# Two transformer layers on one core: another order of the same calls on TensorE, VectorE, ScalarE and GpSimd

## The reference

```
...
        ln_out = layernorm(hidden_states, ln1_s, ln1_b)
        qkv = ln_out @ w_qkv + b_qkv
        q, k, v = jnp.split(qkv, 3, axis=-1)
        ctx = merge_heads(attention(split_heads(q), split_heads(k), split_heads(v), ltor_mask))
        attn_out = ctx @ w_ao + b_ao
        x = hidden_states + attn_out
        ln_out = layernorm(x, ln2_s, ln2_b)
        q = ln_out @ w_q + b_q
        kv = encoder_states @ w_kv + b_kv
        k, v = jnp.split(kv, 2, axis=-1)
        ctx = merge_heads(attention(split_heads(q), split_heads(k), split_heads(v), cross_mask))
        cross_out = ctx @ w_co + b_co
        x = x + cross_out
        ln_out = layernorm(x, ln3_s, ln3_b)
        mlp_out = gelu(ln_out @ w1 + b1) @ w2 + b2
        return x + mlp_out
```

## Time and profile before

| | us |
|---|---|
| median of 3 runs | 1187.67 (1187.09 to 1188.38) |
| the profiled execution, its time | 1188.55 |
| the profiled execution, its span | 1186.8 |
| PE busy | 1050.7 (89%) |
| DVE busy | 815.3 (69%) |
| ACT busy | 509.0 (43%) |
| POOL busy | 434.1 (37%) |

### The profile page before, as it was taken

One profiled execution on the slowest core, in us unless ns is written; L12 is line 12 of the kernel. 1 busy time (PEld: TensorE's weight loads), 2 busy tenths in 40 slices (PEclk: granted clock), 3 DMA queues, 4 the chain that ended last, 5 costly groups with the idle time before them and its releaser, 6 DMA issues. The chain is left out here.

```text
span 1186.8 us, 23743 instructions
## 1 busy us (share of the span) xinstructions
PE 1050.7 (89%) x9056; PEld 714.6 (60%) x9056; DVE 815.3 (69%) x1573; ACT 509.0 (43%) x954; POOL 434.1 (37%) x387
## 2 busy tenths in 40 slices
PE   7988786999999999999999999978996988888866
PEld 5876565668668668668668668656363353443524
DVE  3654776776776776776776866862448787796864
ACT  4643353464364363363373373461231434414331
POOL 2111443442442442442343343331307427264250
PEclk9988888999999999999999999989998999999988
DMA  7130100001002002102101000030000010010100
GB/s 252 62 94 23 41 1 19 24 2 38 24 2 74 23 2 82 36 2 77 55 6 33 24 18 20 9 115 18 1 27 30 1 36 21 0 38 0 36 1 18
DMA packets 38005, 41.14 MB, mean 35 GB/s; under 512 B 8640, under 2 KB 33536, under 8 KB 37648
## 3 DMA queue, kind: packets, MB, share of 16 engines
q1 hardware_dynamic: 37776, 39.54, 10.5%
q0 software_dynamic: 128, 0.10, 0.0%
HBM read 31.25 MB, written 8.39 MB: 33 GB/s over the span
## 5 line engine op out<-in xcount | busy, mean ns | idle before, releaser
L1356 DVE TENSOR_REDUCE b_neg_max<-head_area 128x16 f32<-128x1024 f32 x64 | 77.9, 1218 | 113.9 <-POOL head_area L787 113.5
L2104 POOL TENSOR_TENSOR c_rs<-c_st,head_area 128x512 f32<-128x512 f32 x64 | 88.6, 1416 | 96.8 <-DVE c_st L2583 95.9
L792 POOL TENSOR_TENSOR b_rstd<-b_var,minus_half 128x1 f32<-128x1 f32 x63 | 34.5, 548 | 241.4 <-DVE b_var L1385 241.4
L1207 ACT ACTIVATE head_area<-head_area 128x1024 f32<-128x1024 f32 x64 | 67.9, 1060 | 112.3 <-DVE head_area L1361 111.7
L1039 PE MATMUL ps<-b_hT_mlp,wl 128*128 128x512 f32 x224 | 108.3, 606 | 8.7 <-DVE b_act_g L1407 8.6
L1053 PE MATMUL ps<-w,b_act_g 128*128 128x256 f32 x448 | 104.4, 387 | 2.9 <-ACT b_act_g L1225 2.9
L787 POOL TENSOR_TENSOR head_area<-head_area,b_self_add 128x1024 f32<-128x1024 f32 x32 | 76.7, 2396 | 80.0 <-DVE head_area L1349 80.0
L787 POOL TENSOR_TENSOR head_area<-head_area 128x1024 f32<-128x1024 f32 x32 | 75.5, 2359 | 75.7 <-DVE head_area L1349 75.7
L1212 ACT ACTIVATE head_area<-ps 128x512 f32<-128x512 f32 x128 | 69.9, 598 | 72.5 <-PE ps L986 72.5
L1053 PEld LDWEIGHTS ps<-w,b_act_g 128*128 128x128 f32 x448 | 84.2, 193 | 15.6 <-ACT b_act_g L1225 3.0
L870 PE MATMUL ps<-head_area,wl 128*128 128x512 f32 x176 | 85.5, 609 | 0.0
(11 more groups left out here) (262 smaller groups left out, 2213.1 us busy)
## 6 DMA issues: line engine op xcount, KB each, us to landing
head_area<-x_mid SPq DMA_DIRECT2D x9, 512.0 KB, 3.8
wl<-in_wl SPq DMA_DIRECT2D x4, 1024.0 KB, 6.8
head_area<-in_ctxT SPq DMA_DIRECT2D x8, 512.0 KB, 3.6
x_mid<-b_x_out SPq DMA_DIRECT2D x8, 512.0 KB, 3.6
area<-in_wc SPq DMA_DIRECT2D x1, 2336.0 KB, 8.5
a_x_in<-in_x SPq DMA_DIRECT2D x16, 128.0 KB, 2.9
a_y_in<-in_ctx SPq DMA_DIRECT2D x16, 128.0 KB, 3.4
w<-in_w SPq DMA_DIRECT2D x2, 1024.0 KB, 9.4
```

What stands on the lines that cost most here:

```text
L1356: dve.tensor_reduce(neg_max[:, k % 2, :], t, AX, ALU.max, negate=True).then_inc(max_ok, 1)
L2104: pool.tensor_tensor(rs[:, i % BUFS, :], st[:, i % 3, :], rF[:, i // RS, :], ALU.mult).then_inc(rs_ok, 1)
```

## The change

The `turn` functions of PE, DVE, ACT and POOL keep the same calls with the same arguments, and every wait stays inside its call. Only the order of the calls within a turn differs. The diff, cut to its core (POOL, PE, ACT, DVE):

```
             def turn(n, prev, nxt, entry_of=None):
 
+                add_bias(prev, 6)
+
                 last_inv_std(n, 0, prev)
                 next_add_mask(n, 0, nxt)
-                add_bias(prev, 6)
...
                 next_add_mask(n, 4, nxt)
-                add_bias(n, 2)
+                next_add_mask(n, 5, nxt)
+
+                last_inv_std(n, 5, prev)
+                next_add_mask(n, 6, nxt)
+                add_bias(n, 3)
...
             def turn(n, prev, nxt):
 
+                keys_ctx(n, 0, prev)
+
                 probs_T(n, 0, nxt)
                 last_project(n, 0, prev)
-                keys_ctx(n, 0, prev)
                 times_v(n, 0)
-                next_scores(n, 0, nxt)
                 keys_ctx(n, 1, prev)
                 result_T(n, 0)
+                next_scores(n, 0, nxt)
...
                 times_v(n, 2)
                 next_scores(n, 2, nxt)
+                hidden(prev, 1, nxt)
+                norm_T_mid(n, 1)
                 hidden(prev, 2, nxt)
+                result_T(n, 2)
+                queries_mid(n, 1)
                 hidden(prev, 3, nxt)
-                result_T(n, 2)
-                norm_T_mid(n, 1)
+                last_project(n, 3, prev)
+                hidden(prev, 4, nxt)
...
                 gelu(prev, 0)
                 norm_out_mid(n, 2)
+                norm_out(0, nxt)
+                next_exps(n, 3, nxt)
                 copy_cT(n, 3)
...
-                next_maximum(n, 0, nxt)
-                next_subtract(n, 0, nxt)
+                cross_masks(n)
                 last_residual(n, 0, prev)
                 normalize(n, 0)
+
+                next_maximum(n, 0, nxt)
                 last_norm(n, 0, prev)
+                next_subtract(n, 0, nxt)
                 next_mask(n, 0, nxt)
...
+                next_maximum(n, 3, nxt)
+                last_norm(n, 3, prev)
                 norm_in(nxt if entry_of is None else entry_of)
-
-                next_maximum(n, 3, nxt)
-                pre(prev, 3)
+                pre(prev, 4)
+                pre(prev, 5)
+                normalize(n, 3)
                 next_subtract(n, 3, nxt)
...
+                last_norm(n, 5, prev)
+                last_norm(n, 6, prev)
                 last_norm(n, 7, prev)
...
                 result(prev, 3)
```

More of the change, by code:

```diff
@@ L830, in turn @@
                 add_bias(n, 1)
+                add_bias_in(nxt, 0)
+                add_bias(n, 2)
                 add_bias_in(nxt, 1)
@@ L1117, in turn @@
                 next_scores(n, 4, nxt)
-                queries_in(nxt, 1)
+                keys_in(nxt, 0)
+                norm_T_mid(n, 3)
+                keys_in(nxt, 1)
+                hidden(prev, 6, nxt)
                 result_T(n, 4)
-                norm_T_mid(n, 3)
-                keys_in(nxt, 0)
+                probs_T(n, 5, nxt)
                 queries_mid(n, 3)
-                probs_T(n, 5, nxt)
-                last_project(n, 5, prev)
-                keys_in(nxt, 1)
                 times_v(n, 5)
                 next_scores(n, 5, nxt)
-                hidden(prev, 6, nxt)
-                result_T(n, 5)
+                last_project(n, 5, prev)
                 hidden(prev, 7, nxt)
                 probs_T(n, 6, nxt)
-                last_project(n, 6, prev)
+                result_T(n, 5)
                 values_in(nxt, 0, prev)
@@ L1147, in turn @@
                 mlp_out(prev, 2, nxt)
+                mlp_out(prev, 3, nxt)
                 result_T(n, 7)
-                mlp_out(prev, 3, nxt)
             scores(0, 0)
@@ L1235, in turn @@
                 copy_pT(n, 0)
+                keys(1, n, 0)
+                keys(1, n, 1)
+                copy_cT(n, 0)
                 next_exps(n, 0, nxt)
[L1237 to L1239 removed]
                 copy_pT(n, 1)
+                norm_out_mid(n, 0)
+                norm_out(2, prev)
                 next_exps(n, 1, nxt)
[L1243 to L1244 removed]
                 copy_cT(n, 1)
@@ L1484, in turn @@
                 last_norm(n, 4, prev)
+                next_subtract(n, 4, nxt)
                 next_mask(n, 4, nxt)
+                pre(prev, 6)
                 next_maximum(n, 5, nxt)
                 next_subtract(n, 5, nxt)
+                next_mask(n, 5, nxt)
+                normalize(n, 5)
+                pre(prev, 7)
                 last_residual(n, 5, prev)
-                normalize(n, 5)
-                last_norm(n, 5, prev)
-                next_mask(n, 5, nxt)
-                pre(prev, 6)
                 next_maximum(n, 6, nxt)
-                pre(prev, 7)
                 next_subtract(n, 6, nxt)
-                last_residual(n, 6, prev)
-                last_norm(n, 6, prev)
-                values(0, nxt, 0)
                 normalize(n, 6)
                 next_mask(n, 6, nxt)
+                values(0, nxt, 0)
+                last_residual(n, 6, prev)
+                next_maximum(n, 7, nxt)
                 result(prev, 0)
-                next_maximum(n, 7, nxt)
+                last_residual(n, 7, prev)
+                next_subtract(n, 7, nxt)
                 result(prev, 1)
-                next_subtract(n, 7, nxt)
-                last_residual(n, 7, prev)
+                normalize(n, 7)
+                values(0, nxt, 1)
+                result(prev, 2)
+                next_mask(n, 7, nxt)
+                last_norm(n, 5, prev)
+                last_norm(n, 6, prev)
                 last_norm(n, 7, prev)
-                values(0, nxt, 1)
-                normalize(n, 7)
-                next_mask(n, 7, nxt)
-                result(prev, 2)
                 result(prev, 3)
```

82 lines of the change are left out of this document (34 added, 48 removed).

## The result

The changed kernel takes **1136.36 us** (median of 4 runs, 1134.38 to 1138.02) against 1187.38 for the kernel before (4 runs, 1185.45 to 1188.38): a ratio of 0.9572, 95% interval 0.9548 to 0.9595. The profiled execution took 1138.02 us with a span of 1136.2.

The account below looks back on a forecast made before the run. PE was taken to bound the loop turns, a chain over several engines turns 0 and 7. Gains of 23 (turns 1 to 6), 11 (turn 0) and 6 (turn 7) took 1188.55 to 1148.5, stated as 1148; range 1134 to 1168.

Parts of the forecast that it names:

- The walk through the new order: Hand timing of all four engines through turns 0 to 7, using start-to-start durations from PE; forecast case had chance 0.6.
- Turns 1 to 6, 84.4 each and 23 us counted: Loop turns: 83.2 us dense plus 1.2 of new stalls, against 88.35; 3.8 gained each, 23 us in six.
- tails of the old stalls: Loop turns: the PE call before each of five stalls runs some 0.2 us longer, 1.0 us a turn.
- new stalls: Loop turns: PE waits 0.35 us at `times_v(1)`, 0.4 at `times_v(4)`, 0.05 at `queries_mid(2)`; 1.2 with tails.
- four close calls: Slack under 0.7 us at `probs_T(1)`, `probs_T(2)`, `probs_T(4)`, `mlp_out(0)`; all failing by 0.5 would give back 12 us.
- Turn 0, walk 63 plus 5 for the clock: Turn 0: 63 us at full clock plus 5 for its fall, 68 against 79.4, 11 gained, bounds 4 and 16.
- Turn 7, walk 75.4 plus 5: Turn 7: 75.4 us plus 5 for a low clock, 80.5 against 87.2, 6 gained, bounds 1 and 12.
- Why DVE was late: `norm_in` takes 3.81 us beside POOL's `add_mask`, and `maximum` right behind `mask` waits for `add_mask`: 48 waits, 113.5 us.
- the rival's mechanism, POOL first: Rival "half", chance 0.22: `subtract(3)` loses to POOL's `add_mask` and starts 2.35 us late; 11 us lost in six turns, 1164.
- SP's loads: Costed at nothing: second layer's "middle" weights land near 80 of turn 3, wanted at 83.4; otherwise a few us once.
- more: Rival, chance 0.12: the clock stays up in turns 0 and 7 and some 0.2 stalls count nothing, 1134 us.
- Slower: Rival, chance 0.04: `add_mask` blocks DVE instructions on PE's path three times a turn, 7.05 us a turn; 1200 us.

## Why the prediction came out as it did

The walk through the new order held in all three parts, the reason given for DVE's lateness only in part, and the sum was 10.6 us too small: 40 of the span, 50.6 measured. The three parts together were 14.5 us too small (6.5 in turns 1 to 6, 2.3 in turn 0, 5.7 in turn 7), and 3.9 of that was taken back by the unchanged code around them, which took longer in this profile. The measured time lies near the low end of the stated range. Two of the agreements below hold some luck, and it is named there. Point by point:

- *Turns 1 to 6, 84.4 each and 23 us counted*: 83.43 and 29.5. The difference is 0.95 a turn, 5.7 us in six; another 0.9 went by counting 3.8 where the walk gave 3.95. Two terms were mis-sized. The tails of the old stalls were put at 1.0 a turn; PE's busy time fell by 1.8, from 84.3 to 82.5, so a dense turn is 82.5 and not 83.2. The new stalls were put at 1.2 with tails; PE idles 0.9 a turn, but mostly not where I had it: `times_v(1)` waits 0.25 for 0.35, `times_v(4)` (0.4) and `queries_mid(2)` (0.05) don't wait, and the other 0.67 are the starts of turns, the 1.67 ahead of turn 3 and the 0.70 in turn 1, which the walk didn't have. That 83.2 is so near to the measured turn is luck in this sense. None of the four close calls failed. Two slips in the working: its own figures (1.09 from 0.64) give 1.73 and a wait of 0.28 at `times_v(1)`, not 1.78 and 0.35; and a turn without any stall would gain 6 x 4.95 = 30, not 31.
- *Turn 0, walk 63 plus 5 for the clock*: 63.66 without a fall, 66.10 with one. The walk was right; the clock cost nothing in one of these executions and 2.4 in the other. The stops of 0.7 to 0.9 us that I held to be enough for a fall are there in both, and the fall in the second came ahead of them, in the first 7 us. In the run with `keys_ctx(0)` moved a fall did follow one of them, so the 5 was too much in both executions, but not without ground.
- *Turn 7, walk 75.4 plus 5*: 75.47 at a clock of 1.00. The added 5 failed. The stalls weren't where I put them: `probs_T(4)` 1.30 for 1.5, `mlp_out(0)` 1.03 for 2.1, but `queries_mid(2)` 0.63, `norm_T_mid(3)` 1.11 and `times_v(6)` 0.80 that I didn't have. So the agreement to 0.1 us is luck in part.
- *Why DVE was late*: half right. `norm_in`'s 3.81 us was named as a cause; taken alone it was worth 0.45 us a turn. The pair of `mask` and `maximum` was the cause in the sense that putting three of them back costs 58 us, but four fillers in the old order gave only 1.0 a turn. What was shown is that the new order of DVE loses without the others' (16%), and that with POOL's old order 30 of the 51 us go. What PE's and ACT's moves add, and which of the moves could be left out, was not.
- *`norm_in` 1.4 to 1.6*: 1.38. *Waits for `add_mask` about 50 us*: 24.6. *POOL loses 1.2 at `subtract(3)`*: 0.9, and the rival's mechanism, POOL first, was shown to be real one place further down, though there it cost 3.3 us in six turns and not the rival's 11, with `pre(2)` out of its way. *SP's loads*: the profile puts no stall of PE in these turns down to them.
- *The rivals*: "more" named the clock staying up, which is what happened in turn 7, and its 1134 is the nearer number. "Slower" took DVE's 20 us of spare time as the protection. That argument was wrong: three waits of 2.5 us put back cost 7 us a turn. Of the three blocked instructions that this rival named the new order has one, the `norm` at the end of the turn, 3.50 us instead of 1.2, and it has 15 us of slack.

## What to carry to other kernels

Walk a new order by hand with start-to-start times: it gave 63, 84.4 and 75.4 us where 63.66, 83.43 and 75.47 came, though the single stalls often lay elsewhere, and the largest error was what I added to it for the clock. Judge a wait by the slack at its place, not by an engine's idle share: taking 2.4 us out of `norm_in` gave 0.45 a turn, three waits of 2.5 put back cost 7, and the 2.3 that `norm` loses at the end of the turn gave PE no stall. Engines' orders belong together; DVE's alone lost 16%.

## What was not expected of the hardware

- The unchanged code ahead of turn 0 took between 116.8 and 124.3 us over the profiled executions of these kernels. Windows cut at the same instruction, turn by turn, told more than the totals for differences under 5 us.
- The same order in turn 0, behind the same code, ran at a granted clock of 1.00 once and 0.95 in two other executions: the fall between 124.29 and 135.00 (0.71) isn't decided by the order alone. Nor is a fall behind a stop of 0.7 us, as the two lines of `queries_mid(1)` above show. What decides them stays open.
- A DVE instruction with a single 128x256 SBUF input and an SBUF output (`norm_in`, 1.38 us for four, 3.41 beside `add_mask`) is held up by POOL as `subtract` with two (1.22 and 2.94) is. `norm`, with the same shapes, shows it too: 3.50 for three.
